# Decoder layer with 32 batches in flight: where the ternary weights are prepared, and how the last batch is ordered and placed

## The reference

```python
# self attention, 16 heads of 64, 4 key/value heads, rotary, ALiBi; y = x + attention(x), then normalised
# cross attention on ctx in windows of 64, 16 heads of 16, masked by the cells; normalised before each projection
# feed forward with ternary weights and 8-bit activations:
def _weight_quant(w):
    scale = 1.0 / jnp.clip(jnp.mean(jnp.abs(w)), 1e-05)
    return jnp.clip(jnp.round(w * scale), -1.0, 1.0) / scale
def _act_quant(x):
    scale = 127.0 / jnp.clip(jnp.max(jnp.abs(x), axis=-1, keepdims=True), 1e-05)
    return jnp.clip(jnp.round(x * scale), -128.0, 127.0) / scale
def _bitlinear(x, w):
    return jnp.einsum('bsi,oi->bso', _act_quant(x), _weight_quant(w))
# down(silu(gate(x)) * up(x)) with inner width 1024, added to x, and a last normalisation
```

## Time and profile before

| | us |
|---|---|
| three runs: median (lowest to highest) | 2233.26 (2232.71 to 2235.64) |
| the profiled execution's own time | 2231.77 |
| its span, first to last instruction | 2230.0 |
| PE, DVE, ACT, POOL busy | 2155.6, 1950.3, 1704.1, 1424.6 |

### The profile page before, as it was taken

The page is one execution under the profiler, slowest core; times in us unless marked ns, Lnnn a source line. Parts: engine busy times, 40 slices in busy tenths (PEclk is TensorE's granted clock), DMA queues, the critical chain, the costliest instruction groups (busy, mean ns, idle before and its releaser), DMA issues. The chain is left out here.

```text
span 2230.0 us, 58875 instructions
## 1 busy us (share of the span) xinstructions
PE 2155.6 (97%) x19819; PEld 1671.1 (75%) x19819; DVE 1950.3 (87%) x7968; ACT 1704.1 (76%) x4754; POOL 1424.6 (64%) x1678
## 2 busy tenths in 40 slices
PE   7899999999999999999999999999999999999987
PEld 6677777777787777777777777777777777777755
DVE  5779988999988899998899998889999888999874
ACT  4687778887778888777888777788877788887743
POOL 2566766666776666776666677666667666667631
PEclk9999999999999999999999999999999999999999
DMA  4010111111110110111111111111011101101100
GB/s 164 11 34 25 37 27 33 28 35 28 36 37 23 34 31 25 37 37 30 30 28 36 26 37 37 25 35 28 25 37 37 38 23 28 37 25 37 32 16 10
DMA packets 85400, 74.69 MB, mean 33 GB/s; under 512 B 18544, under 2 KB 79344, under 8 KB 85104
## 3 DMA queue, kind: packets, MB, share of 16 engines
q1 hardware_dynamic: 85104, 70.93, 11.9%
HBM read 45.72 MB, written 8.39 MB: 24 GB/s over the span
## 5 line engine op out<-in xcount | busy, mean ns | idle before, releaser
L1404 POOL TENSOR_TENSOR prob<-prob,precs 128x512 f32<-128x512 f32 x512 | 528.8, 1040 | 561.8 <-DVE precs L1017 557.6
L1312 ACT ACTIVATE prob<-prob,nmax 128x256 f32<-128x256 f32 x1024 | 509.0, 505 | 45.1 <-DVE nmax L1010 45.1
L1010 DVE CUSTOM_DVE_ANT_0 prob<-bank,alibi 128x256 f32<-128x256 f32 x1024 | 371.2, 418 | 23.4 <-PE bank L728 23.1
L1319 ACT COPY pT<-bank 128x512 f32<-128x512 f32 x512 | 303.4, 593 | 55.8 <-PE bank L617 55.5
L617 PE MATMUL bank<-ident,prob 128*128 128x128 f32 x2048 | 316.6, 277 | 4.0 <-ACT pT L1319 3.0
L1336 ACT ACTIVATE px<-px,nmx 128x128 f32<-128x128 f32 x1024 | 313.9, 400 | 4.8 <-DVE nmx L1119 4.8
L617 PEld LDWEIGHTS bank<-ident,prob 128*128 128x128 f32 x2048 | 231.3, 141 | 56.5 <-issue 38.1
L747 PE MATMUL bank<-pT,v_sb 128*64 128x256 f32 x2048 | 249.8, 386 | 3.4 <-DVE qq_lo L1001 3.1
L1119 DVE CUSTOM_DVE_ANT_0 px<-bank,mask 128x128 f32<-128x128 f32 x1024 | 226.3, 286 | 4.8 <-PE bank L807 3.0
L747 PEld LDWEIGHTS bank<-pT,v_sb 128*64 128x64 f32 x2048 | 136.2, 136 | 100.9 <-issue 39.3
L1312 ACT ACTIVATION_READ_ACCUMULATOR prob<-prob,nmax 128x1 f32 x1024 | 199.5, 195 | 0.0
(11 more groups left out here) (216 smaller groups left out, 6028.9 us busy)
## 6 DMA issues: line engine op xcount, KB each, us to landing
raw<-in_xT SPq DMA_DIRECT2D x32, 256.0 KB, 2.9
xtok<-in_x SPq DMA_DIRECT2D x32, 256.0 KB, 2.9
kx_tok<-in_ctx SPq DMA_DIRECT2D x32, 256.0 KB, 3.0
raw<-in_ctxT SPq DMA_DIRECT2D x32, 256.0 KB, 2.9
kx<-k_sin SPq DMA_DIRECT2D x256, 32.0 KB, 2.0
vs<-vx SPq DMA_DIRECT2D x64, 128.0 KB, 2.3
out_y<-x SPq DMA_DIRECT2D x32, 256.0 KB, 3.1
cellk<-in_cell SPq DMA_DIRECT2D x32, 64.0 KB, 3.8
```

Of the source, the lines that this page charges most:

```text
L1010: v.tensor_tensor_reduce(out=prob[:, (2 * p + q) % SLOTS, c, :], in0=psum[SCORES[c]][:, q * L:(q + 1) * L], in1=alibi[:, p % 2, :], scale= ...
L1312: nc.scalar.activation(prob[:, (2 * p + q) % SLOTS, c, :], prob[:, (2 * p + q) % SLOTS, c, :], ACT.Exp, bias=nmax[:, i:i + 1], scale=-1.0, ...
L1319: nc.scalar.copy(pT[:, p % 2, :, :, q * P:(q + 1) * P].rearrange("p c k n -> p (c k) n"), bank[:].rearrange("p (c n) -> p c n", c=4)).then ...
L1404: g.tensor_tensor(prob[:, n % SLOTS, :, :], prob[:, n % SLOTS, :, :], precs[:, 2 * n:2 * n + 2].unsqueeze(2).to_broadcast([P, 2, L]), ALU. ...
```

## The change

The head: the sums of absolute values are three steps of their own on ACT (`sum` 0, 1, 2), put after `qT` 2, after `O` 0 and after `qT` 3 of batch 0. `prep` 6 has only the small instructions, and the nine instructions of the ternary weights are nine steps `ternary` m i on DVE, put between steps from `W` 0 of batch 0 to `Q` 1 2 of batch 1. On PE `prep` 5 moves from ahead of `T` 0 to behind `S` 6. `kx_clear` on POOL moves from between `R` 5 and `R` 6 to between `R` 13 and `R` 14. Three runs of `fill` there are dropped or cut (26 to 0, 15 to 8, 14 to 6 matmuls).

The last batch (31): steps get banks by `home`, from `LAST_BANKS`; cross scores use banks 0 and 1. The order in `TAIL` changes from the end of `OX` 1 of batch 30 on: `KV` 0, `KV` 1 and `KXT` of batch 31 come ahead of `W` 1, `G` and `U` 2 and 3 of batch 30 go between the `SX` steps of batch 31, and `HT`, `D` of batch 30 after `OX` 1 of batch 31. In batch 31 DVE does the copy of `TX` s 1 (ACT did), `X2` and `out` (ACT did), and the sum of `QX`, the shift of `QN` and that of `HS` 1 (POOL did). `x2` and `y3` of batch 31 lie in `px`, POOL leaves out the bias steps of `FS` and `ZS`. The `fill` runs wait for their bank and have other lengths (64 to 42 ahead of `XQ`, 8 to 4 ahead of `D` 1).

```diff
+LAST_BANKS = {("KV", 0): 0, ("KV", 1): 1, ("KXT",): 0, ("NX",): 4, ("QX",): 2, ("QXT",): 4, ("OX", 0): 2, ("OX", 1): 2, ("BX", 0): 0, ("BX", 1): 1,
+              ("NO",): 2, ("PO",): 4, ("HT", 0): 7, ("HT", 1): 4, ("D", 0): 2, ("D", 1): 3}
+LAST_BANKS.update({("TX", s, e): 3 + e for s in range(4) for e in range(2)})
+LAST_BANKS.update({(kind, n): (5, 6, 0, 1)[2 * (n % 2) + (kind == "U")] for kind in "GU" for n in range(4)})
+LAST_XSCORES = (0, 1)
...
 HEAD, "dve":
-        (0, 'qT', 1), (0, 'Q', 0, 2), (0, 'prep', 6), (0, 'Q', 1, 2), (0, 'S', 2), (0, 'prep', 7), (0, 'qT', 2),
-        (0, 'R', 4), (0, 'R', 5), (0, 'S', 3), (0, 'prep', 8), (0, 'R', 6), (0, 'R', 7), (0, 'O', 0), (1, 'K'),
+        (0, 'S', 5), (0, 'R', 10), (1, 'Q', 0, 1), (0, 'R', 11), (0, 'O', 1), (0, 'S', 6), (0, 'prep', 6), (1, 'Q', 1, 1),
+        (0, 'W', 0), (0, 'ternary', 0, 0), (0, 'R', 12), (0, 'R', 13), (1, 'qT', 0), (0, 'ternary', 0, 1), (0, 'S', 7),
+        (0, 'ternary', 0, 2), (0, 'mask'), (0, 'R', 14), (0, 'R', 15), (0, 'O', 2), (0, 'ternary', 1, 0), (1, 'kT'),
+        (1, 'S', 0), (0, 'ternary', 1, 1), (1, 'qT', 1), (0, 'ternary', 1, 2), (1, 'R', 0), (1, 'R', 1), (1, 'Q', 0, 2),
+        (1, 'S', 1), (0, 'ternary', 2, 0), (1, 'R', 2), (0, 'O', 3), (0, 'ternary', 2, 1), (1, 'S', 2), (0, 'ternary', 2, 2),
+        (1, 'Q', 1, 2), (0, 'KV', 0), (1, 'R', 3), (1, 'R', 4), (0, 'W', 1), (0, 'YS'), (1, 'qT', 2), (0, 'KV', 1),
...
 TAIL, "dve":
+        (31, 'KV', 0), (30, 'BX', 0), (30, 'BX', 1), (31, 'KV', 1), (30, 'OS'), (30, 'NO'), (31, 'O', 3), (30, 'PO'),
+        (30, 'FS'), (31, 'KXT'), (30, 'QN'), (30, 'QC'), (31, 'W', 1), (31, 'YS'), (30, 'XQ'), (31, 'NX'), (30, 'U', 0),
+        (31, 'QX'), (31, 'QXT'), (30, 'U', 1), (31, 'SX', 0), (30, 'HS', 0), (31, 'SX', 1), (31, 'TX', 0, 1), (30, 'U', 2),
+        (31, 'SX', 2), (31, 'TX', 1, 1), (30, 'U', 3), (31, 'SX', 3), (31, 'TX', 2, 1), (30, 'HC', 0), (30, 'HS', 1),
+        (31, 'TX', 3, 1), (30, 'HT', 0), (31, 'BX', 0), (31, 'BX', 1), (31, 'OS'), (30, 'HC', 1), (31, 'NO'), (30, 'D', 0),
+        (30, 'HT', 1), (31, 'PO'), (31, 'FS'), (30, 'D', 1), (30, 'ZS'), (31, 'X2'), (31, 'QN'), (31, 'QC'), (31, 'XQ'),
...
-    ternary(0)
-elif n > 6:
-    ternary(n - 6)
+def ternary(m, i):
+    dve.wait_ge(pre_dve, P_CROSSED + 4 + 3 * m + i)
+    if i == 0:
+        v.tensor_scalar(stage[m], stage[m], wrec[:, m:m + 1], MAGIC, ALU.mult, ALU.add).then_inc(pre_dve, 1)
...
+elif kind == "X2":
+    dve.wait_ge(*at("f_rstd", b))
+    for t in range(TT):
+        ins = v.tensor_scalar(x2_last[:, t, :], y2[:, t, :], f_mv[:, t, 0:1], f_rstd[:, t:t + 1], ALU.subtract, ALU.mult)
...
```

More of the change, by code:

```diff
@@ L122 @@
     "pe": [
-        (0, 'fill', 0, 38), (0, 'first', 0), (0, 'first', 1), (0, 'K'), (0, 'fill', 0, 8), (0, 'Q', 0, 1), (0, 'first', 2), (0, 'prep', 1), (0, 'fill', 0, 26), (0, 'prep', 2),
[14 rows of a table removed]
+        (0, 'fill', 0, 38), (0, 'first', 0), (0, 'first', 1), (0, 'K'), (0, 'fill', 0, 8), (0, 'Q', 0, 1), (0, 'first', 2),
+        (0, 'prep', 1), (0, 'fill', 0, 26), (0, 'prep', 2), (0, 'Q', 1, 1), (0, 'fill', 0, 9), (0, 'prep', 3),
+        (0, 'fill', 0, 5), (0, 'qT', 0), (0, 'fill', 0, 24), (0, 'kT'), (0, 'fill', 0, 8), (0, 'S', 0), (0, 'fill', 6, 10),
[14 rows of a table added]
         (2, 'Q', 0, 2), (0, 'BX', 0), (1, 'O', 3), (2, 'T', 0), (0, 'BX', 1), (2, 'Q', 1, 2), (0, 'NO'), (2, 'T', 1),
@@ L328 @@
 EMPTIED.update({("O", u): ("oT_ready", u) for u in range(4)})
+EMPTIED.update({("S", p): ("s_neg", 4 * p + 3) for p in range(PAIRS)})
 EMPTIED.update({("T", n): ("pT_ready", n) for n in range(H)})
@@ L338, with home, xscores, holds @@
 EMPTIED.update({("KV", t): ("vx_ready", t) for t in range(TT)})
-def holds(kind, bank):
-    return bank in (XSCORES if kind == "SX" else SCORES if kind == "S" else (RAW,) if kind in ("load_xT", "load_ctxT") else (BANKS.get(kind),))
+def home(batch, kind, *args):
+    return LAST_BANKS.get((kind, *args), BANKS.get(kind)) if batch == B - 1 else BANKS.get(kind)
+def xscores(batch):
+    return LAST_XSCORES if batch == B - 1 else XSCORES
+def holds(batch, kind, args, bank):
+    if kind in ("SX", "S"):
+        return bank in (xscores(batch) if kind == "SX" else SCORES)
+    return bank == (RAW if kind in ("load_xT", "load_ctxT") else home(batch, kind, *args))
 FILL = max(x[0] for steps in BODY.values() for x in steps) + 1
@@ L355, in freed @@
     for batch, *step in reversed(steps[:n]):
-        if holds(step[0], bank) or (step == ["prep", 5] and bank == 7):
+        if holds(batch, step[0], step[1:], bank) or (step == ["prep", 5] and bank == 7):
+            if batch == B - 1 and step[0] == "TX":
+                _, s, e = step
+                return (sem["pTx_last"], s + 1) if e else (sem["pTx_ready"], batch * COUNT["pTx_ready"] + s + 1)
             name, k = EMPTIED[tuple(step)]
@@ L492, in build @@
         z_neg = sb("z_neg", [P, TT])
+        x2_last = px[:].rearrange("p s h n -> p (s h n)")[:, 0:TT * D].rearrange("p (t n) -> p t n", t=TT)
         y3 = x2
@@ L605, in run @@
                         sp.wait_ge(*at("out_ready", b))
-                        sp.dma_start(one(out_dram, b).rearrange("a p t d -> (a p) t d"), y3[:]).then_inc(sem["stored"], 16)
+                        sp.dma_start(one(out_dram, b).rearrange("a p t d -> (a p) t d"), (x2_last if b == B - 1 else y3[:])).then_inc(sem["stored"], 16)
             run(order("sp"))
@@ L630, in project, with by_token @@
                 return last
-            def by_token(xs, ws):
+            def by_token(bank, xs, ws):
                 parts = ((xs[0], ws[0]), (xs[1], ws[0]), (xs[0], ws[1]))
@@ L637, in by_token @@
                         k, (x, w) = i // 3, parts[i % 3]
-                        last = mm(psum[7][:, t * D:(t + 1) * D], x[:, k, t * P:(t + 1) * P], w[:, k, :], start=i == 0, stop=i == KT * 3 - 1)
+                        last = mm(bank[:, t * D:(t + 1) * D], x[:, k, t * P:(t + 1) * P], w[:, k, :], start=i == 0, stop=i == KT * 3 - 1)
                 return last
@@ L672, in run @@
                     kind, args = step[0], step[1:]
-                    bank = BANKS.get(kind)
+                    bank = home(b, kind, *args)
                     if kind == "first":
@@ L682, in run @@
                         bank, count = args
-                        if bank:
+                        if bank == 6 and b < B - 1:
                             pe.wait_ge(pre_dve, P_CENTRED + 2)
+                        pe.wait_ge(*freed(sem, bank, steps, place))
                         for i in range(count):
@@ L768, in run @@
                         pe.wait_ge(*freed(sem, bank, steps, place))
-                        by_token((yT_hi, yT_lo), (wqx_hi, wqx_lo)).then_inc(sem["QX_mm"], 1)
+                        by_token(psum[bank], (yT_hi, yT_lo), (wqx_hi, wqx_lo)).then_inc(sem["QX_mm"], 1)
                     elif kind == "QXT":
@@ L794, in run @@
                             pe.wait_ge(*landed("kx_filled", b))
-                        pe.wait_ge(*freed(sem, XSCORES[0], steps, place))
-                        pe.wait_ge(*freed(sem, XSCORES[1], steps, place))
+                        pe.wait_ge(*freed(sem, xscores(b)[0], steps, place))
+                        pe.wait_ge(*freed(sem, xscores(b)[1], steps, place))
                         if not second:
@@ L799, in run @@
                                 rows = slice(r * 64, (r + 1) * 64)
-                                last = mm(psum[XSCORES[r]][:].rearrange("p (h n) -> p h n", h=4), qx[rows, g, 0:P], kx[rows, g, :, 0:P],
+                                last = mm(psum[xscores(b)[r]][:].rearrange("p (h n) -> p h n", h=4), qx[rows, g, 0:P], kx[rows, g, :, 0:P],
                                           start=True, stop=True)
@@ L806, in run @@
                                     rows = slice(r * 64, (r + 1) * 64)
-                                    last = mm(psum[XSCORES[r]][i * WIN:(i + 1) * WIN, :].rearrange("p (h n) -> p h n", h=4),
+                                    last = mm(psum[xscores(b)[r]][i * WIN:(i + 1) * WIN, :].rearrange("p (h n) -> p h n", h=4),
                                               qx[rows, g, P + i * WIN:P + (i + 1) * WIN],
@@ L820, in run @@
                             pe.wait_ge(*landed("vs_loaded", b))
-                        pe.wait_ge(*at("pTx_ready", b, 4 * g + 3))
+                        if b < B - 1:
+                            pe.wait_ge(*at("pTx_ready", b, 4 * g + 3))
+                        else:
+                            pe.wait_ge(*at("pTx_ready", b, 2 * g + 1))
+                            pe.wait_ge(sem["pTx_last"], 2 * g + 2)
                         pe.wait_ge(*freed(sem, bank, steps, place))
@@ L841, in run @@
                         pe.wait_ge(*freed(sem, bank, steps, place))
-                        by_token((noT_hi, noT_lo), (wox_hi, wox_lo)).then_inc(sem["PO_mm"], 1)
+                        by_token(psum[bank], (noT_hi, noT_lo), (wox_hi, wox_lo)).then_inc(sem["PO_mm"], 1)
```

(64 more changed lines are left out.)

33 lines of the change are left out of this document (15 added, 18 removed), and 241 rows, old and new, of tables (HEAD, TAIL).

## The result

The changed kernel takes 2238.13 us (median of 20 runs, 2232.49 to 2242.06), the kernel before 2233.07 on the same chip (20 runs): ratio 1.0022, 95% interval 1.0015 to 1.0028, so 3.3 to 6.3 us slower. A second series gave 2238.24 against 2233.62 (1.0020, 1.0011 to 1.0028). The forecast was 2231.5, with a range from 2224 to 2238. The profiled execution of after took 2240.99 us, with a span of 2239.1, so it is 2.9 us above the median.

The account below looks back on a forecast made before the run. PE was taken as the bound (97% busy), with gains left only at the two ends. 2231.77 + 6.5 (head) - 8.3 (tail) = 2230.0, plus 1.5 for the median: 2231.5 us, range 2224 to 2238.

Parts of the forecast that it names:

- rival 4: Clock falls at PE's wait ahead of XQ of batch 30, costing 2 to 3 us: 2234; no separate chance.
- Terms B and C: Head: DVE queue delays from the moved pieces, +5.1 us, and waits on the port shared with POOL, +4.4 us.
- Term A: Head: sums and pieces no longer hold up early steps, so S 5 and T 8 come sooner: -3.0 us.
- DVE well under 19.5: Expected sign in the head: DVE busy well under 19.5 of 20 us in 60:80.
- A + B + C: Head total: earlier steps, DVE queue delays and port waits, -3.0 + 5.1 + 4.4 = +6.5 us.
- Rival 1: Head: POOL lets DVE in and pieces mostly fit, port cost 0: 2227.1 us, or 2222.5; chance 0.32.
- at 19 of 20: Expected sign in the head: DVE busy near 19 of 20 us in 88:120.
- The tail: Last batch: earlier cross scores, QN and feed forward, -8.3 us, bounds -4 to -10.
- rival 3: Last batch: DVE becomes the bound, gain only 4 us: 2235.8, or 2239.1 with higher port cost; chance 0.16.

Follow-up runs that it names:

- tail_only: Kernel before with only the last batch changed and the old head kept: 2226.71 us against 2233.01 (0.9975).
- tail_again: Second measurement of the changed last batch behind the old head: 2224.53 us against 2230.51 for the kernel before (0.9970).
- tail_all: Old head with the changed last batch, plus longer fills in its five longest PE waits: 2224.26 us against 2232.78 for the kernel before.
- head_all_fills: Changed head with the old last batch, plus fills in the head's six longest PE waits: 2236.14 us against 2231.96 for the kernel before.
- whole_all_fills: Changed kernel plus fills in six PE waits of the head and five of the last batch: 2228.22 us against 2230.51 for the kernel before.
- after_again: The changed kernel measured once more, nothing altered: 2238.24 us against 2233.62 for the kernel before.
- head_only: Changed head with the last batch as in the kernel before: 2240.47 us against 2233.01 (1.0042).
- head_again: Second measurement of the changed head with the old last batch: 2240.26 us against 2232.78 for the kernel before (1.0038).
- fills_cut: Kernel before with only its head fills cut as the change cuts them: 2233.29 us against 2233.01.
- pieces_apart: Changed kernel, late clearing, fills except ahead of kT and V, down and up weights' pieces moved later: 2227.84 us against 2231.96 for the kernel before.

## Why the prediction was wrong

**The step that failed** is the one that left the clock out of the sum: a term of 0, where the runs show about 7 us. The prediction named the clock as rival 4, in one place only (ahead of `XQ` of batch 30), at 2 to 3 us, and gave it no chance of its own. With all waits filled the changed kernel takes 2.3 us less than before, where the sum had said 1.8 less (6.5 - 8.3); as it is, it takes 4.6 to 5.1 us more. That the filled kernel comes within 0.5 us of the sum is luck in part: its head alone measured 2.3 us better than forecast (4.2 for 6.5), and what its halves promised did not all come. In the last batch the clock cost 2.2 to 2.5 us (tail_only and tail_again against tail_all). That is rival 4's size, but it took five waits; the one that rival 4 named is not clear of noise alone. The head cost 3.3 us more without fills than with (7.5 against 4.2), and there the prediction had nothing for it, although its Terms B and C themselves made the two longest waits of PE in the head, and although had shown 0.91 in a stretch with a wait of 2.8 us (PE ahead of `O` 0, until 68.8).

**Term A (-3.0)** was right, and lost again as far as the clock fell. In all traces with the new head `T` 0 starts 2.5 us sooner, counted from `Q` 1 2; with the waits filled `T` 8 starts 3.6 us sooner than before, 3.4 from the same count. Without fills it came 0.4 to 3.6 us sooner, by the clock between 60 and 80, as told above. In after its copy came at 87.15 instead of the 83.6 forecast. The mark "DVE well under 19.5" held (6.87).

**Terms B and C (+9.5)** were somewhat too large in sum. In head_all_fills `V` of batch 1 starts 4.7 us later than before and batch 2 5.3 us later, where A + B + C said 6.5; the time said 4.2. The split was off, and so was its ground: "such a DVE instruction does nothing until POOL's run of instructions is over" held only ahead of memsets. The port cost 5.1 us on the pieces (16.15 - 11.07), where 4.4 was priced, but on other ones. `ternary` 0 0 and 1 0, priced at 1.4 us each, lost 0.4 each, since POOL let them in at its first boundary; `ternary` 0 1 slipped through at 1.22 while POOL waited for it (`R` 12 and 13 took 3.06 us against 2.04 in the earlier trace rows), 0 2 took the memsets instead (3.46), and weight 2's pieces, priced at nothing, took 2.30 and 2.17. Rival 1's condition, that POOL lets DVE in between two instructions, was thus met for the most part, and C was not 0 for it. Nor is the 5.1 the price of the move: before had paid 3.8 of it in the old places (14.85 - 11.07). `S` 0 of batch 1 was to come 3 to 4 us later: with the clock kept up it came 0.6 later, in after 7.2 (some 2 of it from the late start of that execution). DVE was never at 19 of 20; its idle time sat in chains with PE and ACT, 3.99 us of it ahead of `S` 0.

**The tail (-8.3)** was right with the clock kept up (-8.5; interval -5.8 to -11.4) and 2.2 too good without. By steps, in tail_all, counted from `SX` 0 of batch 30: `SX` 0 of batch 31 comes 5.8 us sooner (5 forecast), `SX` 3 4.9 on PE and 3.4 on DVE (2.2), `PO` 5.8 (6.3), `XQ` 6.4 (6.65), `G` 3 9.6 (8.05), `D` 1 7.5. The four banks gave 3.2 us instead of 1.4, and more of it was lost at `HT` 0 than the 0.85 allowed (1.6). That DVE would become the tail's bound (rival 3) did not happen; the time of 2238 lies where rival 3 put it, by another cause. No wait of `G` 1 of batch 31 for DVE's freeing of its bank is left.

**What stays open.** The halves measured twice, +7.5 and -6.1, add up to +1.3, the whole measured twice +4.6 and +5.1. The filled halves, +4.2 and -8.5, add up to -4.3, the whole gave -2.3. The intervals of single series are 3 to 6 us wide, so the second gap can be chance; in the trace of whole_all_fills the end gives 5.8 us (from `K` of batch 29 on) where tail_all gives 8.2. The first gap, near 3.5 us, is hard to put down to chance. The traces place it in the head and not in the last batch: from `K` of batch 29 to the end after_again gains 6.2 us and tail_only 6.5, but at that `K` the steps are 12.6 us late in after_again, 11.8 in head_only and 9.0 in head_again. The clock fell for longer there in the whole (0.83 in 120:140) than in the two halves (0.91). Why, with the same steps, is not known.

## What to carry to other kernels

A wait of PE can cost more than its length: where other engines wait for PE, the half clock behind it is added. Before work is moved into a stretch where TensorE is at 19 of 20 us, ask which waits it makes there, and price each with what PE runs right behind it at twice the duration, or fill it. Where PE waits for others anyway, as in fills_cut, the lower clock cost nothing. A sum that comes within 2 us of zero by adding a loss of 9.5 us to gains of 11 is decided by what it leaves out. What a long DVE instruction loses beside a busy POOL depends on its place: over nine pieces 3.8 us in before, 5.1 in the change, 1.1 in pieces_apart. Look first at what POOL runs there, and in what order: moving one step of POOL's, the memsets, gave back 4.2 us of the 4.6 that the change had cost in that series, part of it through the clock.
